# A decoder layer on one core: cross attention's denominators from ones columns beside the value columns

## What is computed

```python
q = jnp.einsum('oc,bct->bot', Wq, target) + bq[None, :, None]
k = jnp.einsum('oc,bcs->bos', Wk, source) + bk[None, :, None]
v = jnp.einsum('oc,bcs->bos', Wv, source) + bv[None, :, None]
# 16 heads of 8 channels; t = s = 256
dot = jnp.einsum('bhdt,bhds->bhts', q, k) / math.sqrt(HEAD_DIM)
dot = mask * dot - (1.0 - mask) * NEG
amap = jax.nn.softmax(dot, axis=-1) * mask
out = jnp.einsum('bhts,bhds->bhdt', amap, v)
return out.reshape(b, HEADS * HEAD_DIM, t)
```

## Time and profile before

| | us |
|---|---|
| median of 3 runs | 974.76 |
| the runs | 969.64, 974.76, 976.74 |
| the profiled execution, its time | 970.83 |
| its span in the trace | 968.9 |
| TensorE busy | 851.0 (88%) |
| VectorE busy | 715.6 (74%) |
| ScalarE busy | 611.9 (63%) |
| GpSimd busy | 537.3 (55%) |

### The profile page before, as it was taken

The page is one execution under the profiler, slowest core; times in us unless marked ns, Lnnn a source line. Parts: engine busy times, 40 slices in busy tenths (PEclk is TensorE's granted clock), DMA queues, the critical chain, the costliest instruction groups (busy, mean ns, idle before and its releaser), DMA issues. The chain is left out here.

```text
span 968.9 us, 22769 instructions
## 1 busy us (share of the span) xinstructions
PE 851.0 (88%) x7883; PEld 556.4 (57%) x7920; DVE 715.6 (74%) x1204; ACT 611.9 (63%) x1028; POOL 537.3 (55%) x671
## 2 busy tenths in 40 slices
PE   3478999999999999999999999988678988959887
PEld 3245766776776677677667667755423444425443
DVE  7768888888888888888888888845566566642255
ACT  3368877877887887788788778732225455543221
POOL 6339769769769769778687694643032213231000
PEclk9989999999999999999999999999759999986799
DMA  6102011011011010010110100000002300000000
GB/s 187 54 1 77 2 34 35 2 33 32 0 32 31 1 32 10 23 32 0 32 32 0 32 11 1 2 1 1 1 1 34 59 2 1 2 27 1 0 22 23
DMA packets 30324, 21.94 MB, mean 23 GB/s; under 512 B 3015, under 2 KB 29319, under 8 KB 30140
## 3 DMA queue, kind: packets, MB, share of 16 engines
q1 hardware_dynamic: 27547, 16.89, 6.0%
q0 software_dynamic: 2720, 4.29, 2.2%
HBM read 22.68 MB, written 1.05 MB: 24 GB/s over the span
## 5 line engine op out<-in xcount | busy, mean ns | idle before, releaser
L961 DVE SCALAR_TENSOR_TENSOR y<-psum,cwh,y 128x508 f32<-128x508 f32 (+2 forms) x384 | 281.6, 740 | 19.6 <-ACT y L679 13.6
L474 POOL TENSOR_TENSOR ct<-lm,levels 128x256 f16<-128x256 f32 x224 | 151.6, 699 | 18.4 <-DVE lm L984 18.4
L460 POOL TENSOR_TENSOR sql<-sq,sqh 128x1024 f16<-128x1024 f32 x32 | 68.3, 2135 | 128.0 <-ACT sq L726 128.0
L679 ACT ACTIVATE y<-psum,cwh 128x512 f32<-128x512 f32 x128 | 99.4, 776 | 52.3 <-PE psum L1223 52.3
L1239 PE MATMUL psum<-wo,vt 128*128 128x256 f32 x512 | 126.0, 389 | 1.2 <-DVE y L961 1.0
L799 ACT ACTIVATE et<-psum 128x1024 f32<-128x1024 f32 x64 | 65.5, 1024 | 58.9 <-PE psum L1534 58.9
L1239 PEld LDWEIGHTS psum<-wo,vt 128*128 128x128 f32 x512 | 92.3, 190 | 11.9 <-DVE y L961 2.0
L1095 DVE TENSOR_REDUCE mx<-psum 128x4 f32<-128x1024 f32 x64 | 77.7, 1221 | 25.9 <-PE psum L1513 25.9
L1223 PE MATMUL psum<-xth,whi 128*128 128x512 f16 x256 | 78.7, 390 | 8.4 <-DVE y L961 5.3
L941 DVE TENSOR_TENSOR ux<-ux,psum 128x512 f16<-128x512 f16 x64 | 43.9, 686 | 53.3 <-PE psum L1321 52.2
L1223 PE MATMUL psum<-xtl,whi 128*128 128x512 f16 x256 | 78.4, 388 | 0.0
(11 more groups left out here) (214 smaller groups left out, 2012.1 us busy)
## 6 DMA issues: line engine op xcount, KB each, us to landing
wraw<-in_L_attn_Wv SPq DMA_DIRECT2D x32, 128.0 KB, 2.7
wo<-in_L_attn_Wo SPq DMA_DIRECT2D x16, 256.0 KB, 2.8
wraw<-in_L_attn_Wk SPq DMA_DIRECT2D x16, 128.0 KB, 2.5
wraw<-in_L_attn_Wq SPq DMA_DIRECT2D x16, 128.0 KB, 2.7
x<-in_x SPq DMA_DIRECT2D x8, 128.0 KB, 4.3
maskrow<-in_mask_row POOLq DMA_DIRECT2D x1, 1024.0 KB, 5.0
xt<-in_ctx SPq DMA_DIRECT2D x1, 1024.0 KB, 6.0
out<-x SPq DMA_DIRECT2D x8, 128.0 KB, 1.8
```

What stands on the lines that cost most here:

```text
L460: g.tensor_tensor(lo, f, hi, ALU.subtract).then_inc(sq_split, 1)
L474: g.tensor_tensor(dst, src, pick.unsqueeze(1).to_broadcast([P, NB, T // (2 * m), m]), ALU.mult).then_inc(masked[l], 1)
L679: s.activation(y[:, n], ubank[n % 2].rearrange("p (j t) -> p j t", j=NB), ACT.Identity, scale=cwh[:, (a.c // 2) % 2, n, TAPS - 1:TAPS], bi ...
L961: v.scalar_tensor_tensor(out=y[:, n, :, sh:], in0=u[:, :, 0:T - sh], scalar=cwh[:, (a.c // 2) % 2, n, TAPS - 1 - sh:TAPS - sh], in1=y[:, n ...
```

## The change

The ones matmuls go. `vz` becomes 32 columns for each strip r and group gq: for even gq eight value columns at 0, for odd gq at 8, and eight ones columns 16 further on. Groups 0 and 1 write columns 0 to 255 of `avb`, groups 2 and 3 columns 256 to 511. So a strip of 32 partitions now has 16 rows of numerators and under them 16 rows of denominators. ScalarE copies all of `avb` to SBUF (`gather`), and SyncE moves the rows with 16 transfers of 16 x 256 (16 KB) per batch into `moved`, eight for the denominators first, eight for the numerators after them. `inverse` takes Ln from `moved`, four units later than `gather`; the copy to `num` goes. `weigh` and `add_x` move to odd h, behind `split_max`, and `widen(h // 2)` stands where `widen(h // 2 + 1)` stood. The memset of `vz` is smaller, `oz` goes, four memsets of ones come, and `widen` is four copies for two. The core of the diff:

```diff
-        vz = fb("vz", [P, 2, 2, 4, 160], F32)
-        oz = fb("oz", [P, 160], F32)
+        vz = fb("vz", [P, 2, 2, 4, 4, 32], F32)
+        avs = fb("avs", [P, 2, 2 * H], F32)
+        moved = fb("moved", [P, 2, 2, H], F32)
...
-            sp.wait_ge(added, STEPS * 2)
-            for n in range(TILES):
-                sp.wait_ge(tapped[n], STEPS * 3)
+            def move_rows(b):
+
+                sp.wait_ge(av_sb, b + 1)
+                need(sp, o_scaled, b - 1)
+                for kind in (1, 0):
+                    for p in range(0, P, 2 * XD):
+                        r, cb = p // 32, p // 16 % 2
+                        sp.dma_start(moved[p:p + 16, b % 2, kind], avs[32 * r + 16 * kind:32 * r + 16 * kind + 16, b % 2, cb * H:(cb + 1) * H]).then_inc((num_moved, den_moved)[kind][b % 2], 16)
+
+            sp.wait_ge(late_set, 2)
+            for b in range(B):
+                move_rows(b)
             sp.wait_ge(xdone, B)
...
                 for st in range(2):
-                    g.tensor_copy(vz[:, b % 2, st].rearrange("p r (g c) -> p r g c", c=40)[:, :, :, 0:XD],
-                                  vv[:, b, st].rearrange("p (r g c) -> p r g c", r=4, c=XD)).then_inc(v_wide, 1)
+                    for e in range(2):
+                        g.tensor_copy(vz[:, b % 2, st, :, e::2, e * XD:(e + 1) * XD],
+                                      vv[:, b, st].rearrange("p (r g c) -> p r g c", r=4, c=XD)[:, :, e::2]).then_inc(v_wide, 1)
...
                 pool.wait_ge(den_masked, b + 1)
-                pool.wait_ge(num_sb, b + 1)
+                pool.wait_ge(num_moved[b % 2], 128 * (b // 2 + 1))
                 need(pool, xdone, b - 1)
-                g.tensor_tensor(oadd[:, b % 2], num[:, b % 2], rmask[:, b % 2], ALU.mult).then_inc(o_scaled, 1)
+                g.tensor_tensor(oadd[:, b % 2], moved[:, b % 2, 0], rmask[:, b % 2], ALU.mult).then_inc(o_scaled, 1)
...
-                if h >= 4 and h % 2 == 0:
-                    weigh(h // 2 - 2)
                 split_max(h)
                 if h % 2 == 0:
                     if h // 2 + 2 < B:
                         mask_x(h // 2 + 2)
-                    if h >= 4:
-                        add_x(h // 2 - 2)
-                    if h // 2 + 1 < B:
-                        widen(h // 2 + 1)
+                    if h >= 2:
+                        widen(h // 2)
+                if h >= 5 and h % 2 == 1:
+                    weigh(h // 2 - 2)
+                    add_x(h // 2 - 2)
...
+            def gather(b):
+                act.wait_ge(o_psum, 4 * b + 4)
+                need(act, den_moved[b % 2], 128 * (b // 2))
+                need(act, num_moved[b % 2], 128 * (b // 2))
+                s.activation(avs[:, b % 2], avb, ACT.Copy).then_inc(av_sb, 1)
+
             def inverse(b):
-                act.wait_ge(o_psum, 4 * b + 4)
+                act.wait_ge(den_moved[b % 2], 128 * (b // 2 + 1))
                 need(act, den_exp, b)
-                s.activation(lden[:], avb[:, H:2 * H], ACT.Ln).then_inc(den_ln, 1)
-                need(act, o_scaled, b - 1)
-                s.activation(num[:, b % 2], avb[:, 0:H], ACT.Copy).then_inc(num_sb, 1)
+                s.activation(lden[:], moved[:, b % 2, 1], ACT.Ln).then_inc(den_ln, 1)
...
                 m = n - LAG - 10
                 if m >= 0 and m % 8 == 0:
+                    gather(m // 8)
+                if m >= 4 and m % 8 == 4:
                     inverse(m // 8)
...
+            gather(B - 1)
             inverse(B - 1)
...
                 for r in range(4):
                     ps = slice(32 * r, 32 * r + 32)
-                    t.matmul(avb[ps, 0:H], vz[:, b % 2, st, r, 32 * gq:32 * gq + 32], et[:, gn % 4, r, st], start=(gq == 0 and st == 0), stop=False, skip_group_check=True)
-                for r in range(4):
-                    ps = slice(32 * r, 32 * r + 32)
-                    mm = t.matmul(avb[ps, H:2 * H], oz[:, 32 * gq:32 * gq + 32], et[:, gn % 4, r, st], start=False, stop=(gq == 3 and st == 1), skip_group_check=True)
+                    mm = t.matmul(avb[ps, gq // 2 * H:(gq // 2 + 1) * H], vz[:, b % 2, st, r, gq], et[:, gn % 4, r, st],
+                                  start=(gq == 0 and st == 0), stop=(gq == 3 and st == 1), skip_group_check=True)
```

More of the change, by code:

```diff
@@ L253, in build @@
         oadd = fb("oadd", [P, 2, H], F32)
-        num = fb("num", [P, 2, H], F32)
         ft = fb("ft", [P, CH, B * T], F32)
@@ L311, in build @@
         x_names = ("x_masked", "q_psum", "q_high", "q_stack", "max_psum", "max_done", "max_scaled", "max_split", "row_psum", "q_full",
-                   "e_psum", "e_done", "o_psum", "den_ln", "den_exp", "den_masked", "num_sb", "o_scaled", "late_set", "v_wide")
+                   "e_psum", "e_done", "o_psum", "den_ln", "den_exp", "den_masked", "av_sb", "o_scaled", "late_set", "v_wide")
         (x_masked, q_psum, q_high, q_stack, max_psum, max_done, max_scaled, max_split, row_psum, q_full,
-         e_psum, e_done, o_psum, den_ln, den_exp, den_masked, num_sb, o_scaled, late_set, v_wide) = [sem(n) for n in x_names]
+         e_psum, e_done, o_psum, den_ln, den_exp, den_masked, av_sb, o_scaled, late_set, v_wide) = [sem(n) for n in x_names]
         f_names = ("ft_psum", "ft_sb", "ftb_sb", "lg_psum", "lg_sb", "lg_max", "lg_exp", "route", "comb_split", "comb_psum", "comb_rows", "sh_psum",
@@ L318, in build @@
          sh_sig, sh_h, gu_psum, gate_sig, gated, cb_psum, he_done, down_done, f_psum, acc_step) = [sem(n) for n in f_names]
+        den_moved, num_moved = [[sem("%s%d" % (n, i)) for i in range(2)] for n in ("den_moved", "num_moved")]
         ubank = [bank[0], bank[1]]
@@ L599, in _ @@
             g.memset(vz[:], 0.0).then_inc(late_set, 1)
-            g.memset(oz[:], 0.0).then_inc(late_set, 1)
-            pool.wait_ge(late_set, 3)
-            g.memset(oz[:].rearrange("p (g c) -> p g c", c=40)[:, :, 0:XD], 1.0).then_inc(late_set, 1)
+            pool.wait_ge(late_set, 2)
+            for e in range(2):
+                for n in range(2):
+                    g.memset(vz[:, n, :, :, e::2, 2 * XD + e * XD:2 * XD + (e + 1) * XD].rearrange("p s r g c -> p (s r) g c"), 1.0).then_inc(late_set, 1)
             widen(0)
@@ L1541, in values @@
                     if gq == 0:
-                        pe.wait_ge(v_wide, 2 * b + 2)
-                        need(pe, num_sb, b)
-                        need(pe, den_ln, b)
+                        pe.wait_ge(v_wide, 4 * b + 4)
+                        need(pe, av_sb, b)
                         if b == 0:
-                            pe.wait_ge(late_set, 4)
+                            pe.wait_ge(late_set, 6)
                 for r in range(4):
                     ps = slice(32 * r, 32 * r + 32)
-                    t.matmul(avb[ps, 0:H], vz[:, b % 2, st, r, 32 * gq:32 * gq + 32], et[:, gn % 4, r, st], start=(gq == 0 and st == 0), stop=False, skip_group_check=True)
-                for r in range(4):
-                    ps = slice(32 * r, 32 * r + 32)
-                    mm = t.matmul(avb[ps, H:2 * H], oz[:, 32 * gq:32 * gq + 32], et[:, gn % 4, r, st], start=False, stop=(gq == 3 and st == 1), skip_group_check=True)
+                    mm = t.matmul(avb[ps, gq // 2 * H:(gq // 2 + 1) * H], vz[:, b % 2, st, r, gq], et[:, gn % 4, r, st],
+                                  start=(gq == 0 and st == 0), stop=(gq == 3 and st == 1), skip_group_check=True)
                 if st == 1:
```

## The result

The changed kernel takes 1003.97 us (median of four runs: 1002.89, 992.60, 1005.05, 1016.14) against 975.60 (four runs) for the kernel before. The ratio is 1.026, with a 95% interval from 1.020 to 1.032: slower, where the prediction said 963.8 us and a range up to 976. The ratio leaves out the slow run of 1016.14 us. The profiled execution took 1002.89 us, its span is 1001.1; against the profiled execution of before that is +32.1.

What follows compares the result with a forecast made beforehand. Cross-attention passes were taken as bound by a 3.25 us chain through other engines plus 5.8 us that TensorE fills alone. Terms -13.8 - 3.0 - 3.4 + 8.2 + 1.0 = -11.0 against the median 974.76 gave 963.8 us, range 955 to 976.

Steps and rivals of the forecast that it cites:

- Clock 1.00 through the stage: Cross attention: sign of a right forecast, TensorE's granted clock reading 1.00 throughout; no term of the sum.
- the clock falls: Cross attention: rival that short TensorE idles lower the clock, 1.55 us a fall, 973.1 or 982.4 us; chance 0.18.
- Matmuls, 0.43 per call: 64 `values` calls lose the second matmul group, 0.43 us each, at most 27.5; three of four save, 1.29 a pass.
- ScalarE on the chain: Query split waits behind ScalarE's other work, 0.27 us per pair of passes; passes become 7.86 us, twelve give -13.8.
- GpSimd's order, -3.0: Around 736 to 760 us: expert loads issued some 8 us earlier, removing a TensorE stall and slow-clock pass, 3.0 us.
- End of the stage, -3.4: After unit 58: 15 calls, 6.4 us of matmul, about half of it saved, 3.4 us (2 to 5).
- Tail, +8.2: After the last `values`: copy, sixteen transfers issued in a row, landing; multiply 8.6 us later, +8.2 net (+2.6 to +10.7).
- Late denominators: ScalarE at `inverse`: rival that landings over 3.5 us delay each batch, slower from 4.9, 982.5 us at 6; chance 0.08.
- Short issues: Last transfers: rival that a 16-row issue costs 0.1 to 0.2 us, 4 to 5.5 us saved, 959.0 us; chance 0.05.
- Another bound in the pass: Cross attention: rival that VectorE's maximum or ScalarE's order makes passes 8.3 us, giving back 5.3, 969.1 us; chance 0.09.

Runs made afterwards that it cites:

- zeros_all: Changed kernel plus a group of four zero-weight fp32 matmuls behind each `values` group, sums unchanged: 980.07 us, ratio 1.005.
- no_ones: Kernel before with only the ones matmuls removed, nothing moved, Ln replaced by a copy times zero (division left out): 1000.52 us, ratio 1.024.
- zeros_b0: Changed kernel plus zero-weight fp32 matmuls in the eight `values` calls of batch 0 only: 1003.08 us, ratio 1.028.
- zeros_half: Changed kernel plus zero-weight fp32 matmuls in every second `values` call: 976.35 us, ratio 1.002.
- zeros_f16: Changed kernel plus one group of zero-weight fp16 matmuls, on `kst`, in each `values` call: 1012.21 us, no ratio.
- holes: Changed kernel plus three groups of four zero-weight fp32 matmuls per pass, placed where TensorE waits for the chain, none in the calls: 964.14 us, ratio 0.992.
- before_order: Kernel before with only `widen(h // 2)` in place of `widen(h // 2 + 1)`, putting batch 2's copies behind the expert loads: 969.97 us, ratio 0.994.
- best: Changed kernel with zero matmuls where TensorE waits, last batch's transfers on two queues, `inverse(6)` behind the last exponentials: 962.84 us, ratio 0.984.

## Why the prediction was wrong

The forecast's sum was -11.0 us, the profiled executions differ by +32.1 and the medians by +28.4. By its own steps:

- *Clock 1.00 through the stage.* This is the step that failed, and it stood in no term of the sum: every duration was taken from rows at 2.4 GHz. The ones matmuls were the work that raised the clock (zeros_all, no_ones), and without them it was lost again (zeros_b0). At 1.2 GHz a pass is 11.35 us, 2.34 over the old one, and twelve of them are 28 us, where the sum had -13.8. A check was at hand: the earlier trace rows has a 7 and a 5 in the slices from 678 to 727 us, just ahead of the full units, and the question "what brings it back up here, and is that what the change removes?" was not asked.
- *The rival "the clock falls".* Right in its subject and wrong in its mechanism and price. It had a fall of 1.55 us for each pass with holes, with a busy TensorE as the argument against. A fall does cost about that when the clock comes back (zeros_half), but in the changed kernel it does not come up at all before the last calls: the price is all of the stage, 2.34 a pass. By that price the rival stood at 963.8 + 12 x (1.15 + 2.34) = 1005.7, where the changed kernel is. With the quoted section on micro-idles in the Trainium skill ("TensorE: Matmul & The Clock Gate") the forecast looked at holes. Here passes with holes keep a full clock (zeros_all, 18.22 of 20 us busy), and a stretch without any has none (zeros_f16, 20.00 of 20). The same page of the Trainium skill, section "What's actually happening", gives the full clock to an engine that has been busy; by the profile's busy time the trace does not agree. The remark of the Trainium skill on that page that transposes don't count as busy in the same way ("Part 4: PE-mode transpose") comes nearer to what these runs show of small matmuls.
- *Matmuls, 0.43 per call, and ScalarE on the chain.* The saving was real where the clock is kept: holes has passes of 7.92 and 8.17 us, 8.05 in the mean, where 7.86 was predicted and "alternating by about 0.2" was said. The 0.19 more may be the fillers' own or ScalarE's; no run takes these apart.
- *GpSimd's order, -3.0.* The hole is gone and the loads are early, as predicted; by itself the edit takes 3.05 us out of three passes of the kernel before (before_order), with medians 5.4 apart and an interval that holds -3.0.
- *End of the stage, -3.4.* Not seen. In holes the last copy starts at 850.78, 12.4 us before the old Ln. Twelve passes 0.96 shorter give 11.5 of it, and GpSimd's order up to 3 more, so the end of the stage gave nothing back, or cost up to 2. Part of that is ScalarE's wait for batch 6, 2.75 us in holes, where half a microsecond was allowed; part may be the clock, which rose a little later (0.63 in 730 to 732).
- *Tail, +8.2.* Counted from the last copy it was +10.3, where the working has 8.6 (8.2 after 0.4 for the shorter last call). The size of the issue was off. The line below gives the issues by tile (min/median/max ns): 0.59 at the median, 0.62 with the gap, where 0.47 had been read from loads of 128 rows and 0.5 was set as the upper end. Fifteen of 0.15 more are 2.3. The landing, 1.8 at the median, was 0.5 under the 2.3 taken. The tail as a whole stayed within its own bound of +10.7.

```profile
L401 SPq DMA_DIRECT2D moved<-avs x128: 507/589/1849, 748.6 to 901.6; - x128
```

- *Late denominators.* Right that they aren't: the eight Ln of `lden` wait once for a transfer, 6.2 us in all, and that is the tail. Where passes are short, in holes, batch 6 waits too. *Short issues* falls. *Another bound in the pass* falls too as a cause: TensorE idles 0.20 us in a pass of 11.35.

What stays open: how much matmul work is needed to raise the clock and how much to hold it (half of the filler was nearly enough), whether the amount or the 128-row form of the matmuls decides, why the clock rises up to 6 us later in one execution than in another, why one of four runs of the changed kernel, of no_ones and of zeros_f16 lies 9 to 20 us under the others, and the 6 us of the last stage.

## What to carry to other kernels

Before counting what a removed matmul saves, ask what clock the stage starts at and which work raises it: where a stretch begins at 1.2 GHz, less work can cost all of the time that it saves and more. "TensorE busy 98%" is no evidence for a full clock, so read the granted clock of each stage beside it, before and after. If useful work can't hold the clock, zero matmuls put where the engine waits for others anyhow can (964 us against 1004 here), while the same fillers in the stretch that TensorE fills give back what was won (980).

## What the runs showed of the hardware

- The granted clock did not follow the busy time: 0.50 with 20.00 of 20 us busy (zeros_f16) and with 156.87 of 160 (the changed kernel), 1.00 with 16.17 of 18 (before). What told the kernels in which it rose from those in which it did not was the second group in the `values` calls or its filler. One fp32 group of four 32-column strips and four fp16 groups of the same size did the same, one fp16 group did not; zeros did the same as ones.
- The last stage lasts 96.5 to 96.8 us after the addition to x in the changed kernel, in zeros_f16 and in holes, and 101.6 to 103.9 in the ten other profiled executions. Between the kernel before and the changed one the difference is one more fall of the clock some 40 us in. The ten us from there, first of the kernel before, then of the changed one:

```profile
905.86:915.86 10.00, 9.34 (x25) 6.32 (x26) 2.98 (x5) 0.85 (x2) 0.00 (x0) 0.57 0.00 0
```

```profile
944.28:954.28 10.00, 9.50 (x47) 5.74 (x48) 4.16 (x7) 2.26 (x4) 0.00 (x0) 1.00 0.00 0
```

  The same instructions get through 25 matmuls in one and 47 in the other. Since runs of one kernel scatter by as much (955 and 963 in best), I take it for chance of the execution; no run tests that.
- SyncE issues a transfer of 16 rows of 1 KB within the chip's SBUF every 0.62 us, and it lands 1.8 us after its issue (median), 3.4 at the latest in zeros_all.
